# Attention steps of a PixArt block dealt out by the tiling of the TensorE array

## The reference

```
for layer in (0, 1):
    xn = layernorm(x)
    q, k, v = xn @ Wq.T + bq, ctx @ Wk.T + bk, ctx @ Wv.T + bv      # split in 16 heads
    s = (q @ k.T) * tau[batch] + delta[batch, key]
    x = x + (softmax(s / 4) @ v) @ Wo.T + bo
    xn2 = layernorm(x)
    layer 0: scores = sigmoid(xn2 @ router.T); choose 4 of 8 groups, then 8 of 64 experts;
             x = x + sum_e coef_e * (silu(xn2 @ Wg_e) * (xn2 @ Wu_e)) @ Wd_e + shared expert
    layer 1: softmax(xn2 @ Wg.T); 2 of 8 experts of width 704; the same form, no shared expert
```

## Time and profile before

| what | value |
|---|---|
| timed runs, median of 3 | 1362.74 us (1360.32 to 1367.02) |
| span of the profiled execution, first to last instruction | 1311.0 us |
| PE, PEld busy | 1221.2 us (93%), 949.1 us (72%) |
| DVE, ACT, POOL busy | 829.9 us (63%), 495.5 us (38%), 539.5 us (41%) |
| score rows (line 627) | 1024 instructions, 526 ns each |
| mean granted TensorE clock | 0.971 |

### The profile page before, as it was taken

The page is one execution under the profiler, slowest core; times in us unless marked ns, Lnnn a source line. Parts: engine busy times, 40 slices in busy tenths (PEclk is TensorE's granted clock), DMA queues, the critical chain, the costliest instruction groups (busy, mean ns, idle before and its releaser), DMA issues. The chain is left out here.

```text
span 1311.0 us, 40484 instructions
## 1 busy us (share of the span) xinstructions
PE 1221.2 (93%) x12894; PEld 949.1 (72%) x12895; DVE 829.9 (63%) x2657; ACT 495.5 (38%) x1255; POOL 539.5 (41%) x691
## 2 busy tenths in 40 slices
PE   5999999999977999999879999999999889999995
PEld 3666666666645988888556666666666889999995
DVE  3468777787767666666475777787865444444442
ACT  2454545454421434344224545554543121222121
POOL 1135656656473001100476676766522213333331
PEclk9999999999979999999979999999996999999998
DMA  4334444446545678865333333333324113354322
GB/s 113 104 118 145 133 148 137 144 134 203 152 136 184 200 203 235 262 187 160 105 87 91 99 104 101 93 101 97 87 56 181 54 38 101 100 161 115 101 35 81
DMA packets 115803, 166.65 MB, mean 127 GB/s; under 512 B 26480, under 2 KB 96768, under 8 KB 114672
## 3 DMA queue, kind: packets, MB, share of 16 engines
q0 software_dynamic: 22672, 58.41, 16.6%
q1 hardware_dynamic: 46496, 54.35, 14.3%
q10 hardware_dynamic: 46560, 52.98, 12.5%
HBM read 87.82 MB, written 63.49 MB: 115 GB/s over the span
## 5 line engine op out<-in xcount | busy, mean ns | idle before, releaser
L1047 DVE TENSOR_REDUCE mx<-banks 112x2 f32<-112x750 f32 x256 | 235.9, 936 | 93.1 <-PE banks L627 79.6
L1898 POOL DMA_INDIRECT xs_d<-xns,idx x160 | 155.6, 973 | 159.9 <-PE banks L653 113.9
L1567 ACT ACTIVATE shared_buf<-banks 125x672 f32<-125x672 f32 x256 | 173.1, 728 | 99.3 <-PE banks L653 98.2
L1912 POOL DMA_INDIRECT kept<-y_d,yidx x128 | 125.5, 980 | 115.4 <-issue 86.7
L919 PEld LDWEIGHTS banks<-xT,attn_buf 128*128 128x128 f32 x1364 | 158.7, 194 | 5.1 <-DVE xT L1433 3.6
L919 PE MATMUL banks<-xT,attn_buf 128*128 128x128 f32 x1364 | 159.0, 277 | 3.4 <-DVE xT L1433 3.4
L864 PE MATMUL banks<-xT,staged 128*128 128x128 f32 x1064 | 142.6, 277 | 7.1 <-DVE staged L1444 6.8
L864 PEld LDWEIGHTS banks<-xT,staged 128*128 128x128 f32 x1064 | 129.2, 192 | 11.9 <-DVE xT L1433 8.2
L653 PE MATMUL banks<-attn_buf 18*125 18x112 f32 x3072 | 121.5, 288 | 11.1 <-DVE mx L1047 6.4
L2064 POOL DMA_INDIRECT acc<-shared_buf,ids x31 | 57.9, 1866 | 166.9 <-ACT shared_buf L1798 127.4
L653 PEld LDWEIGHTS banks<-attn_buf 18*125 18x125 f32 x3072 | 98.7, 188 | 36.4 <-issue 18.0
(11 more groups left out here) (214 smaller groups left out, 1959.7 us busy)
## 6 DMA issues: line engine op xcount, KB each, us to landing
shared_buf<-xs_d SPq DMA_DIRECT2D x136, 128.0 KB, 2.4
y_d<-shared_buf ACTq DMA_DIRECT2D x132, 128.0 KB, 2.5
ringbuf<-in_we SPq DMA_DIRECT2D x6, 2176.0 KB, 8.2
ringbuf<-in_we POOLq DMA_DIRECT2D x32, 384.0 KB, 4.6
attn_buf<-attn_buf SPq DMA_DIRECT2D x128, 93.8 KB
attn_buf<-in_ctxT ACTq DMA_DIRECT2D x29, 375.0 KB
xs_d<-zrow ACTq DMA_DIRECT2D x16, 512.0 KB
y_d<-zrow ACTq DMA_DIRECT2D x16, 512.0 KB
```

What stands on the lines that cost most here:

```text
L1047: dve.tensor_reduce(mx[:, i % 2, 2 * p:2 * p + 2], banks[0:Q, 2 * p:2 * p + 2, 0:S], AX.X, ALU.max).then_inc(s_max, 1)
L1567: act.activation(pT[:, slot:slot + 2, :], banks[0:KT, first_bank:first_bank + 2, 0:ST * Q], ACT.Exp, scale=0.25).then_inc(s_exp, 1)
L1898: pool.indirect_dma_start(xs_d[L.number], bass.IndirectOffsetOnAxis(ap=idx[:, b % 2, k:k + 1], axis=0), rows, None).then_inc(s_scat[b % 2] ...
L1912: pool.indirect_dma_start(yg[:, u, k, :], None, y_d, bass.IndirectOffsetOnAxis(ap=yidx[:, u, k:k + 1], axis=0)).then_inc(s_gat[u][k * 4 // ...
```

## The change

The step is put in another order. Transposed scores now use banks 4 to 7 (`ROWS_T`) and come first; the score rows of quad i+2 follow at once; then come all full-array jobs of the step, each with a bank of its own from 4 to 7 and each waiting for the half of the exponential that frees this bank; then PV of the same quad i (bank 0) and the turned maximum of quad i+2 (bank 1). Transposed scores wait for the evictions of the full-array jobs of the step before. `V01` becomes `V0` and `V1`. The two filler matmul pairs of step 1 in layer 0 go. VectorE's lists are written anew, POOL applies layer 1's first normalisation ahead of two gathers, and some table values are loaded one by one with a check of bounds.

```diff
+        def counts(handle, row, first, count, top):
+            return [handle.value_load(tabr[0:1, row, bass.ds(first + k, 1)], min_val=0, max_val=top) for k in range(count)]
...
-        BETWEEN = (("XT", 2),), (("O2T", -1),), (("RK", -2),), (("V2", 1),)
-        BEHIND = ((("Q", 2), ("OT", -1)), (("V01", 1), ("OP", -1)), (("K0", 2), ("XT2", -1)), (("K1", 2), ("LG", -1)))
+        FULL = ((("OT", -1, 4), ("V2", 1, 5), ("XT", 2, 6), ("V0", 1, 7)),
+                (("O2T", -1, 4), ("Q", 2, 5), ("OP", -1, 6), ("V1", 1, 7)),
+                (("K0", 2, 5), ("RK", -2, 4), ("XT2", -1, 6)),
+                (("K1", 2, 4), ("LG", -1, 5)))
-        SCORES_T = (4, 5, 0, 1)
+        ROWS_T, OUT_BANK, MAX_BANK = 4, 0, 1
-        FILL_SCORES = (4, 6, 0, 0), (0, 0, 0, 0)
+        FILL_SCORES = (0, 4, 0, 0), (0, 0, 0, 0)
@@ TensorE, scores_T @@
-                    elif l == 0 and i == 1:
-                        idle(2, bank[SCORES_T[0]])
@@ TensorE, body @@
+                        scores_T(n, u, i, b, taken)
+                        if rows_ahead:
+                            score_rows(*ahead, (s_mev, n * NQ + (i + 2)))
+                        taken = []
+                        for j, r, k in jobs_of(l, b)[i]:
+                            if runs(l, j, b, r):
...
+                                job(j, n + r, (u + r) % 2, bank[k], [(s_exp, n * (2 * NQ) + (2 * i + (1 if k < 6 else 2)))], l=1 if next_layer(l, j, b, r) else l)
+                                taken.append((ev[j], n + (r + 1)))
...
+                        pv(n, u, i, rows_ahead)
+                        if rows_ahead:
+                            max_T(ahead[0], ahead[2], MAX_BANK)
@@ VectorE, layer 0 @@
-                    WORK = ((("MAX", 0), ("R0", -2), ("W81", -3), ("OT", -1)),
-                            (("R1", -2), ("MAX", 0), ("R2", -2), ("R3", -2), ("OP", -1), ("MOM2", -1)),
-                            (("RK", -2), ("MAX", 0), ("MOM", 3)),
-                            (("SLOT", -2), ("MAX", 0), ("R4", -2), ("W80", -2)))
+                    WORK = ((("OT", -1), ("MAX", 0), ("R0", -2), ("R1", -2)),
+                            (("MAX", 0), ("OP", -1), ("MOM2", -1), ("R2", -2), ("R3", -2)),
+                            (("MAX", 0), ("RK", -2), ("MOM", 3), ("R4", -2)),
+                            (("MAX", 0), ("SLOT", -2), ("W80", -2), ("W81", -2)))
@@ VectorE, layer 1 @@
-                    WORK = ((("MAX", 0), ("C0", 3), ("C1", 3), ("OT", -1)),
-                            (("R1", -2), ("R2", -2), ("MAX", 0), ("C2", 3), ("OP", -1)),
-                            (("MOM2", -1), ("RK", -2), ("MAX", 0), ("LN2", -1), ("C3", 3), ("MOM", 3)),
-                            (("SLOT", -2), ("MAX", 0), ("R3", -2), ("W80", -2), ("W81", -2), ("R0", -1)))
+                    WORK = ((("OT", -1), ("MAX", 0), ("C0", 3), ("C1", 3)),
+                            (("MAX", 0), ("OP", -1), ("MOM2", -1), ("R1", -2), ("R2", -2), ("C2", 3)),
+                            (("MAX", 0), ("RK", -2), ("LN2", -1), ("C3", 3), ("MOM", 3)),
+                            (("MAX", 0), ("SLOT", -2), ("R3", -2), ("W80", -2), ("W81", -2), ("R0", -1)))
@@ ScalarE, body: both halves of the exponential, the step's evictions, out_ev(n, i), max_ev of quad i + 2 @@
+                        exp(n, i, 0)
+                        exp(n, i, 1)
+                        for j, r, k in jobs_of(l, b)[i]:
...
+                        out_ev(n, i)
+                        if i < 2:
+                            max_ev(n, i + 2)
+                        elif in_layer(b, 1):
+                            max_ev(n + 1, i - 2)
@@ SP, body: key rows first, then maximum rows 2, 3 and 0 of the next batch, query rows, maximum row 1 @@
@@ ScalarE, POOL, SP: context loads behind V1 (were behind V2); apply ahead of gather(b + 4, b % 2, 6, 2) in layer 1 @@
-                    needs = table_values(SP, 2, first, EDGE, L.E)
+                    needs = counts(sp, 2, first, EDGE, L.E)
@@ VectorE, experts of layer 1 @@
-                    return list(zip(cols, table_values(DVE, 2, first, count, L.E)))
+                    return list(zip(cols, counts(dve, 2, first, count, L.E)))
```

More of the change, by code:

```diff
@@ L522, in tiles1 @@
                     for s in range(L.ring):
-                        done = table_values(SP, 3, i * L.ring + (TT // 2 + s), 1, L.tiles + 1)[0]
+                        done = counts(sp, 3, i * L.ring + (TT // 2 + s), 1, L.tiles + 1)[0]
                         sp.wait_ge(s_dn[1], done)
@@ L548, in _ @@
         def _(pe):
-            M0, M1 = bank[6], bank[7]
             pe.wait_ge(s_con, 32)
@@ L622, in score_rows @@
                         pe.wait_ge(s_delta[u], (n - u) * 8 + 16)
-                    wait(pe, s_max, g * 2)
-                    wait(pe, s_exp, g * 2 - 5)
+                    wait(pe, *free)
                     for j in range(QUAD):
@@ L697, in first @@
                             shared_down(3, {2: (ev["Q"], n + 1), 3: (ev["XT"], n + 1)})
-                            free = [[(s_sev, 4 * 4 + SEV_CREDIT - 1)], [(s_sev, 4 * 4 + SEV_CREDIT)]]
+                            free = {k: [(s_sev, 4 * 4 + SEV_CREDIT - 3 + k - 4)] for k in range(4, 8)}
                         elif j == "FILL":
-                            idle(r, bank[SCORES_T[0]])
+                            for sm, v in free[k]:
+                                wait(pe, sm, v)
+                            idle(r, bank[k])
@@ L789, in last @@
                         idle(13)
-                    job("RK", n, 1, [(ev["LG"], n + 1)])
+                    job("RK", n, 1, bank[4], [(ev["RK"], n)])
                     if l:
@@ L1068, in job @@
                     elif j == "RK":
-                        link(after().tensor_tensor(key[:, 0:E], bank[7][0:Q, 0:E], run[0:Q, 0:E], ALU.add))
+                        link(after().tensor_tensor(key[:, 0:E], bank[4][0:Q, 0:E], run[0:Q, 0:E], ALU.add))
                         after().tensor_tensor(key[:, 0:E], key[:, 0:E], sel[:, 0:E], ALU.mult)
-                        link_signal(dve.tensor_tensor(run[:, 0:E], run[:, 0:E], bank[7][:, E:2 * E], ALU.add), ev[j], n + 1)
+                        link_signal(dve.tensor_tensor(run[:, 0:E], run[:, 0:E], bank[4][:, E:2 * E], ALU.add), ev[j], n + 1)
                     elif j == "SLOT":
@@ L1275, in last @@
                     weights = "R4" if l == 0 else "R3"
-                    order = ([("W81", -2)] if l == 0 else []) + [("OT", 0)] + [(j, -1) for j in route_of[l:]] + [("OP", 0), ("MOM2", 0), ("RK", -1), ("LN2", 0)]
+                    order = [("OT", 0)] + [(j, -1) for j in route_of[l:]] + [("OP", 0), ("MOM2", 0), ("RK", -1), ("LN2", 0)]
                     order += [("SLOT", -1), (weights, -1), ("W80", -1)]
@@ L1984, in body1 @@
                     after_scores(n, 3)
+                    if in_layer(b, 3):
+                        apply(0, n + 3, b + 3)
                     if in_layer(b, 4):
```

337 lines of the change are left out of this document (140 added, 197 removed).

## The result

| | before | changed |
|---|---|---|
| median of 5 runs | 1362.98 us (1360.32 to 1372.88) | 1492.52 us (1483.59 to 1498.14) |
| ratio | | 1.0942, 95% interval 1.0901 to 1.0983 |
| span of the profile | 1311.0 us | 1481.4 us (that run took 1483.59) |
| mean granted clock | 0.971 | 0.906 |

The forecast was 1355, range 1338 to 1376. The kernel before takes 1312 to 1315 us in some sets of runs (first kind) and 1363 to 1371 us in others (second kind), one and the same chip has shown both, and its profile fits the first kind while its timed runs belong to the second.

What follows compares the result with a forecast made beforehand. TensorE's own order of work was taken as the bound. Layer 0 -17.9, layer 1 +12.1 and openings -2 net -7.8 on the 1311.0 us span; with 51.7 kept on top, 1355 us, range 1338 to 1376.

Steps and rivals of the forecast that it cites:

- Layer 1, step 2: XT2 on TensorE waits 2.1 us for VectorE's late LN2, making layer 1's batch 0.93 us longer.
- T + 5.6: Layer 1, step 2: predicted start of XT2, T being the start of the step.
- 20.05 + 2.1: Layer 1's batch: TensorE's own work of 20.05 us plus the wait for LN2, giving 22.15.
- Queues: DMA queues: SP's maximum rows come in time and POOL keeps pace with 20 us a batch; nothing added.
- T + 1.77: Front of each step: first full-array job starts 1.77 us after step start T, released by the exponential's first half.
- the gain of 1.28: Layer 0's attention: each batch falls from 21.33 to 20.05 us, -17.9 over 14 batches.
- Single loads of table values: Experts' loads on VectorE and SP, one value at a time: put at 0, high end 10 us.
- the new wait: Front of each step: first full-array job waits for the exponential's first half, 0.1 to 0.3 us.
- the 51.7 us: Median of the timed runs above the profiled span of 1311.0; kept unchanged in the forecast.
- A: VectorE becomes the bound in both layers, late maxima holding back PV and turned max: 1378 us, chance 0.2.
- B: Layer 1's wait for LN2 stays small: 1327 us, or 1343 with the on-time wait of 1.2; chance 0.12.
- C: Pairs don't share a tiling, or the back costs 1.06: +17 us at most, 1364, no change; chance 0.18.

Runs made afterwards that it cites:

- e4: The changed kernel as it is, run again in a set of the first kind: 1373.5 us, ratio 1.0447.
- e17: Changed kernel with 12 filler matmuls ahead of XT2 in layer 1's step 2, without most of attention's indirect DMAs: 1343.7 us, ratio 1.0229 (unclear).
- e1: Kernel before with only its loads of table values written in the changed form, first kind of set: 1321.4 us, ratio 1.0069.
- e10: Changed kernel with 12 filler matmuls ahead of XT2 in layer 1's step 2, second kind of set: 1485.7 us, ratio 1.0830.
- e16: Changed kernel with LN2 ahead of the maximum, zero rows behind the evictions, most of attention's indirect DMAs left out: 1301.1 us, ratio 0.9902.
- e18: Changed kernel, all DMAs kept, LN2 ahead, zero rows behind the evictions, GpSimd's share released by the second exp: 1310.6 us, ratio 0.9988.
- e6: Kernel before with the changed table loads and two idle semaphores more, shifting the later numbers: 1322.7 us, ratio 1.0046.
- e7: Changed kernel with GpSimd's share of each attention step released by the second exp instead of the transposed scores: 1377.2 us, ratio 1.0442.
- e12: Changed kernel without most of attention's indirect DMAs, in a set of the second kind: 1390.7 us, ratio 1.0177 (unclear).
- e3: Changed kernel without most of attention's indirect DMAs, in a set of the first kind: 1367.7 us, ratio 1.0395.
- e13: Kernel before with only its table loads in the changed form, in a set of the second kind: 1371.5 us, ratio 1.0045.
- e2: Kernel before with the changed table loads and without most of attention's indirect DMAs, first kind of set: 1311.8 us, ratio 0.9969.
- e14: Separate kernel of signals alone, TensorE handing small matmuls to ScalarE beside GpSimd's DMAs, second kind of set: streaming row tiles up to 1.96 us late.
- e8: Changed kernel with LN2 moved ahead of the maximum in layer 1's step 2, second kind of set: 1477.9 us, ratio 1.0771.
- e15: Changed kernel with LN2 ahead of the maximum and zero rows behind the evictions, second kind of set: 1468.8 us, ratio 1.0761.

## Why the prediction was wrong

Of the 129.5 us between the two kernels in the measured set, 60.7 are what the order costs in a set of the first kind, and the other 68.8 are what it costs more in one of the second. Two steps of the prediction failed for the first part, one for the second.

*Layer 1, step 2: the wait right, its price not.* XT2 was to wait about 2.1 us, and does: 2.10 in e4, where it starts at T + 5.73 against the predicted T + 5.6. **The step that failed is the one behind it: the batch was summed as 20.05 + 2.1, every later row at the full clock.** TensorE stands 2.1 us, then runs at 1.2 GHz (granted clock 0.50), and step 3 takes 6.90 instead of the predicted 4.48 (e17, same wait filled: 4.41). A batch is 25.4 in e4, not 22.15. Layer 1 came out at +58.7 us (395.8 against e1's 337.1, each in one profile), not +12.1. The Trainium skill, "TensorE: Matmul & The Clock Gate", section "HAM oscillation — how this bites in real kernels", tells of a kernel whose TensorE waits in each tile and starts each next one at half clock, half of that time being lost; here the waits are shorter, and e10 and e17 agree with the mechanism.

*Queues: ScalarE's was left out.* **The second step that failed is the term for the queues.** The prediction went through SP's and POOL's queue and had nothing for the DMA issues on ScalarE's. The load of the context moved from V2 in step 3 to V1 in step 1, where the two issues of zero rows already stood, and together they hold two evictions. Layer 0's step 2 is 5.85, predicted 4.70; e16 and e18 have 5.08 and 5.11 with two of the three moved; the 0.4 that is left lies with the same two, which now stand ahead of step 2's exp:

```profile
229.17 0.92 PE L662 MATMUL banks<-attn_buf 18*125 18x112 f32 x24
229.43 0.40 ACTq L1638 DMA_DIRECT2D xs_d<-zrow  x1
230.02 0.40 ACTq L1641 DMA_DIRECT2D y_d<-zrow  x1
230.52 1.35 ACT L1556 ACTIVATE shared_buf<-banks 125x672 f32<-125x672 f32 x2 [0.99 <-PE banks L662]
```

That is e16 in order of time, TensorE and ScalarE: the exp starts 1.35 behind the scores, not 0.98, and ScalarE's queue ends its last issue at 230.42. The profile names TensorE as releaser; by the times I take it to be the queue. The other steps of layer 0 came as worked out: 5.26, 5.61, 4.45 against 5.16, 5.71, 4.48, and the first full-array job is released at T + 1.77 (231.10 to 232.87). Where nothing disturbs it, e4's batch is 21.2, so the gain of 1.28 is just eaten by the 1.15 of step 2. That is the median, and layer 0 as a whole came out at +15.4 us (347.3 against 331.9), not -17.9: four batches take 24.9, 23.0, 27.2 and 23.7, the waits of step 2 being longer in them (the fourth issue in the third), and step 3 then takes 6.1 to 7.4 instead of 4.45. So the two prices meet: in the first and the third of these the granted clock of step 3 is 0.54 and 0.50, behind waits of 1.32 and 2.30 for the maximum's row.

*Single loads of table values.* They were put at 0. e1 and e6 show some 6 to 10 us, most of it on SP's side in layer 0's experts; behind the last scores, where VectorE's four loads lie, e1's profile is 1.5 longer (295.4 against 293.9).

*Together* these make the first kind of set: 4.5% slower, where -0.6% was forecast. e18 undoes the two failed terms, with GpSimd's share released later as in e7, which alone changed nothing, and is level with the kernel before.

*The new handoff has no cover.* "This is the new wait: 0.1 to 0.3 in each step" took the signal's travel as constant. The wait was priced, the cover that goes with it was not: before, TensorE had full-array jobs between the scores and whatever needs the exp. This is the step that failed for the second part. In sets of the second kind the changed kernel takes 119 us more (1492.5 against e4's 1373.5) and the kernel before 50 to 56. Of the changed kernel's 119, 23 are left without attention's indirect DMAs (e12 against e3); the rest comes and goes with them and their late signals. That the order pays more for them is seen in layer 0's attention alone, 40.6 against 7.1 us (the profiles show some 39 of the 68.8 us, the changed kernel's first being of its fastest run and e4's of its slowest); that the missing cover is the reason is read from the traces of two batches, and no run puts the cover back. That moving the scatters avoids it is not shown either (e18). The prediction could not know of late signals, since its profile was from a set without them, but it had the 51.7 us as a hint.

*The 51.7 us around the span.* They are not around the span: each later run lies 1.7 to 2.2 us above its own. Profile and timed runs came from sets of different kinds, and e13, a kernel like before in a set of the second kind, has a span of 1369.5.

*Rivals.* A: VectorE did not become the bound; in the page above TensorE ends 171.3 of the 218.2 us of idle time ahead of the maxima. Its place shows only where the scatters are left out: in layer 0's step 0 the turned maximum then waits up to 0.5 for VectorE in some batches, and that step is 5.58 in e3 and 5.59 in e16 instead of the 5.26 and 5.27 of e4 and e18; why there was not looked into. B, layer 1's wait undone, was to bring 20 to 36 us against before; e16 brings 11 (1301.1 against the 1312.4 of its set; 9 by the ratios of e16 and e2), less than that, since each layer gains 5 us (326.8 against e1's 331.9 and 332.0 against 337.1) and not 17.9 and 16. C: the back took 0.88 in e4 (PV's first matmul 230.22, the next scores 231.10) against the 0.90 worked out, and the pairs share a tiling. No rival had the size that came: A, 15 us over no change, also put every row at the full clock.

## What to carry to other kernels

A wait that TensorE didn't have before can have two prices: its length, and what the half clock adds to the work behind it. Look for the second in the granted clock behind each such wait; a filler that keeps the clock can be worth placing even where it delays the job a little. A median batch can hide both prices: compare the whole stage as well. When a step is re-dealt, walk every engine's queue with its DMA issues, also ScalarE's and the batches with an issue more, and list for each handoff what TensorE can still do if the answer comes a microsecond late. And compare a profile's own time with the timed runs first: 50 us between them is a finding, not a constant.

## What the runs showed of the hardware

In some sets of runs TensorE's semaphore changes came up to 2.9 us behind its matmuls' ends beside GpSimd's indirect DMAs; away from them none was over 0.3 us but a few of 0.4, which sets of the first kind have too. VectorE's and ScalarE's were not looked at in the same detail. e14, one execution, shows it on bursts of row tiles and not on single full-array matmuls; why is open. The Trainium skill, "NOTIFIC — the notification-queue block", section 7.1 "Overflow: three behaviours, one of which stalls the engine", says that this block, which carries the trace's records, always backpressures in its internal pipeline rather than lose a record inside. Bursts of small matmuls make the most records here: 24 in 0.92 us for the scores, 4 in 1.53 us for K1. The profiles with late signals also lack more records: of VectorE's 2657 instructions that change a semaphore, they hold 2360 to 2405 changes, those of the first kind 2635 to 2685 and e12, without attention's indirect DMAs, 2608. Each run here carries a trace or clock record, so no run tells whether recording has a part. What makes a set of the second kind is open too: chip 5 was of the first kind in e4 to e7 and of the second in e8 to e15.
